# The last feed-forward's routing and sends moved into the attention ahead of it, its shared expert moved beside the gathers

## What is computed

```
# L3 attention: two mambas, one over the reversed sequence
u, z = split(x @ in_w.T);  u = silu(conv(u));  dbc = u @ xproj_w.T
dt = softplus(dbc[:64] @ dt_w.T + dt_b);  Bm, Cm = dbc[64:80], dbc[80:96]
h = exp(dt * A) * h + (dt * u) * Bm        # over time, 256 channels x 16 states
y = (h . Cm + u * D) * silu(z) @ out_w.T
# L3 feed-forward: 16 experts, 2 per token, at most CAP = 640 tokens each
probs = softmax(x @ router_w + router_b);  vals, idx = top_k(probs, 2)
pos = place of the token in its expert's queue;  within = pos < CAP
out = x + mlp(x, shared) + sum_k vals_k * within_k * mlp(rows, expert idx_k)
mlp(h) = (silu(h @ wg) * (h @ wu)) @ wd     # 176 hidden features
```

## Time and profile before

| | us |
|---|---|
| median of 3 runs | 3957.37 (3955.27 to 3960.35) |
| the profiled execution | 3963.04 |
| its span, first to last instruction | 3961.3 |
| PE busy | 3420.1 (86%), granted clock 0.943 of full |
| DVE, ACT, POOL busy | 2411.4 (61%), 1850.6 (47%), 1703.2 (43%) |
| last attention | 2589.0 to 3537.1 |
| last feed-forward | 3538 to 3943.2 |

### The profile page before, as it was taken

One profiled execution on the slowest core, in us unless ns is written; L12 is line 12 of the kernel. 1 busy time (PEld: TensorE's weight loads), 2 busy tenths in 40 slices (PEclk: granted clock), 3 DMA queues, 4 the chain that ended last, 5 costly groups with the idle time before them and its releaser, 6 DMA issues. The chain is left out here.

```text
span 3961.3 us, 70814 instructions
## 1 busy us (share of the span) xinstructions
PE 3420.1 (86%) x24832; PEld 2293.2 (58%) x24832; DVE 2411.4 (61%) x5406; ACT 1850.6 (47%) x5019; POOL 1703.2 (43%) x1869
## 2 busy tenths in 40 slices
PE   6888897769999899999988999879999999973781
PEld 3555554547777566666653444357777777762560
DVE  3788843446666556666643444458888888863233
ACT  4666655466666444454450000266666666620220
POOL 2555522337777633333310000146676667645106
PEclk7999998889999999999998999989999999986895
DMA  4888730030000000000016877512222222241112
GB/s 134 211 215 213 205 90 10 6 68 1 1 2 2 1 1 2 2 1 2 2 44 139 154 150 153 111 51 77 76 76 71 79 76 76 71 133 46 48 68 63
DMA packets 266184, 289.98 MB, mean 73 GB/s; under 512 B 60841, under 2 KB 177513, under 8 KB 265578
## 3 DMA queue, kind: packets, MB, share of 16 engines
q1 hardware_dynamic: 259146, 271.80, 27.5%
q0 software_dynamic: 4096, 8.40, 0.7%
q10 hardware_dynamic: 2592, 5.26, 0.3%
HBM read 233.21 MB, written 52.17 MB: 72 GB/s over the span
## 5 line engine op out<-in xcount | busy, mean ns | idle before, releaser
L2232 DVE TENSOR_TENSOR_SCAN a_h<-a_dA,a_dBu_psum 128x512 f32<-128x512 f32 x512 | 595.9, 1205 | 162.6 <-issue 105.9
L2189 POOL TENSOR_TENSOR a_h<-a_h,main_g 128x512 f32<-128x512 f32 x256 | 383.6, 1501 | 269.6 <-DVE a_h L2232 259.5
L1237 POOL TENSOR_SCALAR a_probs<-a_probs,a_row_inv 128x128 f32<-128x128 f32 (+1 forms) x512 | 380.0, 763 | 178.0 <-DVE a_row_inv L1200 178.0
L1703 DVE SCALAR_TENSOR_TENSOR m_hidden<-m_h_psum,m_gate_spread 128x512 f32<-128x512 f32 x256 | 176.8, 691 | 264.7 <-PE m_h_psum L1641 252.2
L1956 PE MATMUL a_dBu_psum<-a_B_diag,a_dt_u_turned 64*128 64x128 f32 x4096 | 316.9, 289 | 20.5 <-DVE a_h L2232 19.7
L1506 POOL TENSOR_TENSOR r_position_q<-r_turned_q 128x512 f32<-128x512 f32 x128 | 159.7, 1268 | 389.3 <-DVE r_turned_q L1551 389.3
L179 POOL TENSOR_TENSOR main_g<-main_g,main_s 128x512 f32<-128x512 f32 x28 | 41.2, 1503 | 632.1 <-ACT main_g L161 632.1
L1956 PEld LDWEIGHTS a_dBu_psum<-a_B_diag,a_dt_u_turned 64*128 64x128 f32 x4096 | 257.8, 188 | 74.5 <-issue 69.5
L1463 ACT ACTIVATE r_probs<-r_logits_psum,r_neg_max 128x256 f32<-128x256 f32 x512 | 235.0, 475 | 140.0 <-DVE r_neg_max L1557 140.0
L1142 ACT ACTIVATE a_probs<-a_logits,a_neg_max 128x128 f32<-128x128 f32 (+1 forms) x512 | 226.7, 446 | 127.0 <-DVE a_neg_max L1186 127.0
L1977 PE MATMUL a_y_psum<-main_ident,a_h 128*128 128x128 f32 x2048 | 274.9, 276 | 7.7 <-POOL a_h L2189 6.6
(11 more groups left out here) (519 smaller groups left out, 7659.0 us busy)
## 6 DMA issues: line engine op xcount, KB each, us to landing
m_gate_spread<-m_gate_rows SPq DMA_DIRECT2D x64, 1024.0 KB, 8.3
main_g<-a_b_c_rows SPq DMA_DIRECT2D x256, 256.0 KB, 3.1
a_band_rows<-main_g SPq DMA_DIRECT2D x64, 512.0 KB, 3.7
a_B<-a_band_rows SPq DMA_DIRECT2D x192, 128.0 KB, 3.4
a_A<-a_band_rows SPq DMA_DIRECT2D x192, 128.0 KB, 3.2
f_x_rows<-f_zero ACTq DMA_DIRECT2D x16, 320.0 KB, 8.6
f_x_expert<-f_x_rows SPq DMA_DIRECT2D x16, 320.0 KB
f_y_rows<-f_y_expert SPq DMA_DIRECT2D x16, 320.0 KB, 2.2
```

Source lines behind the costliest of these rows:

```text
L1237: ins = nc.gpsimd.tensor_scalar(pr[:, h % NPR, tile[t]], pr[:, h % NPR, tile[t]], rinv[:, p % NST, q:q + 1], None, ALU.mult)
L2189: tt(h[:, r, :, :], h[:, r, :, :], Cs[:, g % NCS, :, :], ALU.mult).then_inc(hc_pool, 1)
L2232: nc.vector.tensor_tensor_scan(flat, dA[:, M % NDA, q, k, :, :].rearrange("p n t -> p (n t)"), db[:, 2 * (g % 2) + k, :], 0.0, ALU.mult, A ...
```

## The change

Routing moves ahead. The router's logits are made by PE at the end of `gate_and_norm`, behind its last tile; picking and placing are DVE's first work in the attention block, ahead of the first scan; their tables lie in buffers that the attention needs from its second unit on. PE turns the tokens there, and SP writes them to DRAM (`x_tok`). SP clears the slots and reads the tokens back tile by tile, and POOL issues one send in three steps from step 26 on. The product with B's weights (`b_proj`) becomes `turn_b`, which turns B from `low`, the copy that ACT has made of the projection.

In the feed-forward the experts come first, with weights loaded in parts of four experts, and the rows of the next chunk are turned before the products of this one. The 16 shared chunks stand last; after every second one, DVE combines four tiles of gathered rows. The third layer's `rpe_bias` is loaded before SP's other loads.

```diff
@@ -245,9 +245,16 @@
+                    if beside and "tensor" in beside:
+
+                        pe.wait_ge(logged, N)
+                        for k in range(N):
+                            pe.wait_ge(normed, k + 1)
+                            beside["tensor"](pe, k, *own)
...
+                also("sync_first", sp)
@@ -976,8 +983,10 @@
...
+            def load(sp, rpe_in, *_):
+                sp.dma_start(rb[:], d["rpe_bias"]).then_inc(rpe_in, 16)
             def spread(sp, rpe_in, zeroed, padded, summed, ready, rows_out, bias_in, *_):
-                sp.dma_start(rb[:], d["rpe_bias"]).then_inc(rpe_in, 16)
...
+        def table(a):
+            return a.rearrange("p (t e) -> p t e", t=NT)
+        probs, eq = table(dt[1][:, 0, :]), table(dt[1][:, 1, :])
+        chosen = [table(dtu[1][:, k, :]) for k in range(TOPK)]
+        run = [table(zs[1][:, k, :]) for k in range(2)]
+        both, slot = (table(dtuT[1][:, q, :, :].rearrange("p c e -> p (c e)")) for q in range(2))
...
+            nc.vector.tensor_tensor(probs, table(rt[:, 0, :]), rb[:].unsqueeze(1).broadcast_to([P, NT, E]), ALU.add)
...
+        def router_logits(pe, k, weights_in, A_exp, flip_zero, log_mm):
+            if k == 0:
+                pe.wait_ge(weights_in, 16 * len(pairs))
+            for n in range(4 * k, 4 * k + 4):
+                ins = nc.tensor.matmul(rt[:, 0, n * E:(n + 1) * E], xn[:, n * P:(n + 1) * P], rw[:], start=True, stop=True,
+                                       skip_group_check=True)
+            if n == NT - 1:
+                ins.then_inc(log_mm, 1)
...
+        FIRST_CLEAR, FIRST_SCATTER, EVERY = 2, 26, 3
...
-                def b_proj(N):
+                def turn_b(N):
...
+                    pe.wait_ge(low_sb, N + 1)
                     for q in range(2 * TC):
-                        for k in range(NK):
-                            ins = mm(pj[:, 1, q * NS:(q + 1) * NS], u[:, k, q * P:(q + 1) * P],
-                                     W[N % 2]["xp"][:, k, DR:DR + NS], start=k == 0, stop=k == NK - 1)
+                        ins = mm(pj[:, 1, q * NS:(q + 1) * NS], low[:, q * P:(q + 1) * P],
+                                 c["ident"][0:DR + 2 * NS, DR:DR + NS], start=True, stop=True)
...
@@ -1965,6 +2024,8 @@
                     if m == 0:
                         if U:
                             pe.wait_ge(gated, 2 * (U - 1) + q + 1)
+                        else:
+                            pe.wait_ge(counted, 1)
...
+                def turn_tokens(m):
+                    if m >= 4:
+                        pe.wait_ge(lo_taken, m - 3)
+                    for n in range(4):
+                        ins = nc.tensor.transpose(db[:, m % 4, n * P:(n + 1) * P], xn[:, (4 * m + n) * P:(4 * m + n + 1) * P],
+                                                  c["ident"][:])
+                    ins.then_inc(turned_mm, 1)
+
+                def count():
+                    pe.wait_ge(picked, 1)
+                    flat = both.rearrange("p t e -> p (t e)")
+                    mm(yT[:, 0, :], c["earlier"][:], flat, start=True, stop=True)
+                    mm(yT[:, 1, :], c["ones"][:], flat, start=True, stop=True).then_inc(count_mm, 1)
...
+                for m in range(4, NG4):
+                    turn_tokens(m)
                 low_proj(0)
-                b_proj(0)
+                turn_b(0)
...
+                count()
+                pe.wait_ge(hi_taken, NG4 - 4)
...
+                def put_tokens(half):
+                    sp.wait_ge((lo_taken, hi_taken)[half], 4)
+                    src = h[:, 4 * half:4 * half + 4, :, :].rearrange("p r n t -> p (r n t)").rearrange("p (n f) -> p n f", f=P)
+                    sp.dma_start(x_tok[16 * half:16 * half + 16].rearrange("n p f -> p n f"),
+                                 src).then_inc((tokens_lo, tokens_hi)[half], 16)
+
+                def clear(e):
+
+                    sp.dma_start(route.slots(route.x_rows, e),
+                                 zero[:].unsqueeze(1).broadcast_to([P, PER, P])).then_inc(cleared, 16)
+                def take_row(n):
...
+                    if n >= NROW:
+                        sp.wait_ge(scattered[n % NROW], 16 * TOPK * (n // NROW))
+                    sp.dma_start(rows[:, n % NROW, :], x_tok[n]).then_inc(row_in[n % NROW], 16)
+
+                put_tokens(0)
...
+                    if g == NCS:
+                        put_tokens(1)
                     read_c(g)
+                    if FIRST_CLEAR + NCS <= g < FIRST_CLEAR + NCS + E:
+                        clear(g - FIRST_CLEAR - NCS)
+                    ahead = g - FIRST_SCATTER + 2 * TOPK * EVERY
+                    if ahead >= 0 and ahead % (TOPK * EVERY) == 0 and ahead // (TOPK * EVERY) < NT:
+                        take_row(ahead // (TOPK * EVERY))
...
+                def scatter(i):
+                    n, k = i // TOPK, i % TOPK
+                    if i == 0:
+                        pool.wait_ge(cleared, 16 * E)
+                    pool.wait_ge(row_in[n % NROW], 16 * (n // NROW + 1))
+                    nc.gpsimd.indirect_dma_start(route.x_rows, bass.IndirectOffsetOnAxis(ap=dest_u[:, n, k:k + 1], axis=0),
+                                                 rows[:, n % NROW, :], None).then_inc(scattered[n % NROW], 16)
...
                     times_c(g)
+                    if g >= FIRST_SCATTER and (g - FIRST_SCATTER) % EVERY == 0 and (g - FIRST_SCATTER) // EVERY < NT * TOPK:
+                        scatter((g - FIRST_SCATTER) // EVERY)
...
+                def pick():
+                    link(reduce(out=first[:], in_=probs, axis=AX_X, op=ALU.max))
+                    link(tt(probs, probs, per_tile(first[:]), ALU.subtract))
...
+                    tt(both, chosen[0], chosen[1], ALU.add).then_inc(picked, 1)
...
                     dve.wait_ge(dbu_mm, 2 * (g + 1))
+                    if g == 0 and k == 0:
+                        dve.wait_ge(tokens_lo, 16)
+                    if g == 2 and k == 0:
+                        dve.wait_ge(tokens_hi, 16)
...
+                pick()
+                for m in range(4, NG4):
+                    take_tokens(m)
+                place()
...
+                def turn(i):
+                    e, t, n = chunks[i]
+                    if t == 0:
+                        pe.wait_ge(x_in, 16 * (e + 1))
+                    if i >= 2:
+                        pe.wait_ge(turn_sb, i - 1)
+                    for k in range(n):
+                        ins = nc.tensor.transpose(tr[:, i % 2, k * P:(k + 1) * P], xe[:, e % NX, t + k, :], c["ident"][:])
+                    ins.then_inc(turn_mm, 1)
 
...
+                    if t == 0 and (e % PART == 0 or e == E):
+                        pe.wait_ge(loaded[e // PART], 16 * 3)
+                    if i < NSL:
+                        pe.wait_ge(turn_sb, i + 1)
+                        rhs = xeT[:, i % NXT, 0:w]
+                    else:
                         rhs = xn[:, t * P:t * P + w]
...
+                def turn_back(m):
+                    if m >= 2:
+                        pe.wait_ge(added, m - 1)
+                    for n in range(4 * m, 4 * m + 4):
+                        pe.wait_ge(combined, n + 1)
+                        ins = nc.tensor.transpose(tr[:, m % 2, (n % 4) * P:(n % 4 + 1) * P], acc[:, n % NG, :], c["ident"][:])
+                        ins.then_inc(back_mm, 1)
+
+                turn(0)
                 for i in range(NCH + 1):
+                    if i + 1 < NSL:
+                        turn(i + 1)
                     if i < NCH:
                         raise_(i)
                     if i >= 1:
                         lower(i - 1)
+                        if quad(i - 1) is not None:
+                            turn_back(quad(i - 1))
...
+                def combine(n):
+                    dve.wait_ge(gathered[n % NG], 16 * TOPK * (n // NG + 1))
+                    if n >= NG:
+                        dve.wait_ge(back_mm, n - NG + 1)
...
+                def add(m):
+                    dve.wait_ge(back_mm, 4 * m + 4)
+                    dve.wait_ge(o_sb, NSL + 2 * m + 2)
...
+                        m = quad(i - 1)
+                        if m is not None:
+                            for n in range(4 * m, 4 * m + 4):
+                                combine(n)
+                            if m >= 1:
+                                add(m - 1)
...
+                def load(part):
+                    es = slice(part * PART, (part + 1) * PART)
...
+                load(0)
                 for e in range(E + 2):
                     if e < E:
                         take_rows(e)
+                    if e % PART == 0 and e // PART + 1 < E // PART:
+                        load(e // PART + 1)
+                    if e == E - PART:
+                        load_shared()
                     if e >= 2:
                         put_rows(e - 2)
```

388 lines of the change are left out of this document (180 added, 208 removed).

## The result

The changed kernel takes 3869.38 us (3866.61 to 3872.01, 4 runs), the kernel before beside it 3958.86 (3955.27 to 3964.64): a ratio of 0.9773, 95% interval 0.9756 to 0.9789. It is faster, as forecast, but by half of what was forecast: the profiled spans are 3867.0 and 3961.3 us, a gain of 94.3 for 193, and 3869 lies outside the range of 3732 to 3812. Of the runs further on, one execution of `free_steps_again` took 8374.27 us at a granted clock of 0.413; it is left out of that kernel's ratio, but not of its median.

A forecast was written before the change was run, and what follows sets the result against it. PE was taken to bound the last attention, a serial DVE chain or POOL's indirect DMAs the routing, sends and gathers. Terms summed to -193.2 on the profiled 3963.0, so 3769.8, less 5.7 for the median: 3764 us, range 3732 to 3812.

The forecast's parts named there:

- Part 6: Last attention: 64 sends beside the scans, 16 of them in POOL's way at 0.6 us each; +9 us (0 to +40).
- the upper end of 40: Last attention: worst case for the sends beside the scans, +40 us, half of the 80.6 they add on POOL.
- Rival (b): Last attention: sends are on the path, any slip of POOL passed on; 80.6 us rather than 9, total 3835; chance 0.08.
- Rival (c): Last attention: each send holds up ACT and DVE some 11 us, 717 us added, about 4470, slower than before; chance 0.03.
- Parts 2 to 5: Third layer's load first -14 us, last norm +4.5, way to the first scan +12.5, B turned from ACT's copy -14.7.
- part 4: Way to the first scan: picking hidden in DVE's idle; PE's chain 29.8 us, then placing 14.0, scan at 44.2; +12.5 us.
- Rival (d): Before the first scan: routing isn't hidden as DVE's picking starts late; +31 us rather than +12.5, total 3783; chance 0.07.
- The experts' period: Feed-forward: an expert takes 7.1 us in place of 9.12, since turning one chunk ahead removes PE's waits; 16 take 113.8.
- Part 1: Feed-forward after the attention: 126.7 us until the first gather, gathers 88 with the shared expert hidden, tail 18.1; -190.5 us.
- rival (a): Gather stretch: PE at half clock beside the gathers, period 13.5 us, stretch 111 in place of 88, total 3787; chance 0.17.

The follow-up runs named there:

- free_steps_again: Changed kernel with sends ahead of POOL's product with C at steps 1, 3, 5, 7, 9, gathers as changed, run again for comparison: 3773.09 us, ratio 0.9574.
- sends_free_steps: Changed kernel with sends moved ahead of POOL's product with C, at steps 1, 3, 5, 7, 9 from the third unit on: 3789.36 us, ratio 0.9565.

## Why the prediction was right in sign and wrong in size

*Part 6, the sends beside the scans, is the step that failed.* It asked where a send stands in POOL's way, and priced 16 of the 64 at 0.6 us. That question was answered rightly as far as POOL goes: the memset in the send's place costs 13.5, not far from 9. It never asked what a send does to an instruction of DVE that starts beside it. The trace of before had no such pair with POOL going straight on: beside its gathers DVE's second combining instruction (L2559), with two inputs in SBUF, starts while an indirect DMA is issued in 30 of 32 tiles and takes its 0.35 us in all of them, but POOL stands still for some 0.30 us behind every gather. So the upper end of 40 ("the latter half of the 80.6") was a bound for the wrong mechanism. The cost is 82.6, and it isn't spread: 26 of 256 products carry 78 us more than their usual time, and over the attention PE stands still 49 us longer and, at a lower clock, works 34 us longer. The forecast had no term for either.

*Rival (b)* had the right size (80.6, total 3835) and 0.08, for another reason: POOL's load. `sends_free_steps` tells them apart, with POOL at 77% and no loss. *Rival (c)* spoke of stalls of other engines by single sends, with 3.2 us a send as the point where the change turns slower. 82.6 / 64 = 1.3 is well under it, so the sign was safe. What I held against it, that the first nine sends delayed nothing, looked at ACT and DVE instructions that read PSUM; the held ones read SBUF only.

The Trainium skill, "SBUF — State Buffer", section "Who interferes with whom", has a rule that bears on this: a DVE instruction with two inputs in SBUF contends with a GpSimd instruction that reads SBUF. Of DVE's two-port modes it says that whoever issues first has the shared ports for the whole instruction and blocks the other. The 1.71 beside the memset's follower agrees with both. The measured holds behind a send go further: they last for a whole run of POOL's instructions (4.25 us over three). The held one-input multiplication may or may not be a case of the rule, since the section counts `tensor_scalar` among the operations that can take both ports; in turned order it takes 0.68 us in the median, against 0.43 for one of the same size in plain order (2618.43 in the changed kernel). I had not brought the rule to bear, and it would have asked the right question.

*Parts 2 to 5* came out within 1.7 us each: -13.0, +6.0, +13.4, -13.0 (part 4's own terms, 29.8 and 14.0, add up to 43.8 and not to its 44.2). Rival (d) is out: DVE's picking was hidden in the idle before the scans, and only placing stood bare. Two errors nearly cancelled there. PE's chain was through 26.8 us after the start for the 29.8 I wrote, and placing took from 2608.8 to 2627.1, 18.3 us for 14.0. The reason is in single rows, of the kernel before and of the changed one:

```profile
3583.01 0.17 DVE L2503 COPY f_running<-f_running 128x16 f32<-128x16 f32 x1
```

```profile
2609.61 1.16 DVE L2406 COPY a_silu_z<-a_silu_z 128x16 f32<-128x16 f32 x1
...
2617.04 0.29 DVE L2406 COPY a_silu_z<-a_silu_z 128x256 f32<-128x256 f32 x1
```

The same small copy takes 1 us more while POOL works (on dt and the first diagonals, to 2616.6), and the next three take 0.8 to 1 us more (1.13, 0.97, 1.00); the fifth, behind POOL's run, is at its 0.29 of before. The section just named counts copies among the operations that can contend with POOL, and here the trace agrees. The experts' period was 7.44 for 7.1.

*Part 1, the gathers*: the floor was right and the reading of the stretch was not. Where handoffs are on time, the 64 gathers, unchanged, take 85.2 to 86.4 us in four profiles, with the lower clock in it, for the 88 forecast:

```profile
3748.00:3834.00 86.00, 59.97 (x202) 39.04 (x200) 39.42 (x102) 8.30 (x14) 61.48 (x64) 0.81 0.19 49
```

(the changed kernel, run again). PE is at 0.81 there, the pairs of chunks start with four gate matmuls of 1.37 to 1.91 us for 1.03, and the 10 us of POOL hide it: rival (a)'s mechanism is there and costs nothing. The 12.2 us over the forecast in the first profile come from the late handoffs that the earlier trace rows had shown at the sends. I had argued them away for the gathers because none showed beside those of before, where ACT and PE hand nothing to each other that could be late. Why the handoffs were late stays open: the runs say that the same kernel has them in some sets of runs and not in others, and no more.

By the sum: 75.3 from the sends, 12.2 from the gathers, 5.5 before the first gather, and 5.9 from the small terms together, of a miss of 98.9.

## What to carry to other kernels

An indirect DMA put beside a tuned pipeline can cost more than its own time on POOL, if POOL goes straight on behind it while DVE starts on data in SBUF: put it where POOL must wait anyway, here ahead of a product that waits for DVE. Move it with the data of one period in hand, step by step, and look at the longest instructions of the *other* engines, not at the mean or the load. And before a cure is judged, the unchanged kernel is run beside it on the same chip, since a delay of 27 us was there in some sets of runs and not in others.

## What the runs showed of the hardware

- A product of DVE (0.67 us) that starts while POOL issues an indirect DMA, or in the unbroken run of POOL instructions behind it, ended some 0.56 us after that run: 2.80 to 6.97 us in the changed kernel. A memset of 1.06 us in the DMA's place gives at most 1.80; a one-column memset behind it leaves as many (27 long for 26 and 27); behind a standstill of 0.07 us or more none was held; one input in place of two, in turned order, does not help (31 long).
- Where PE stood still for 3.86 us behind a held product, the granted clock was 0.68 and 0.75 in the next two stretches of 3 us, and four matmuls of 512 columns took 3.49 us for 1.98. Over the attention this adds 34 us to PE's busy time (881.7 for 847.7).
- A small copy of DVE in SBUF (128x16) takes 0.17 us alone and 1.16 beside a working POOL. An indirect DMA takes POOL 0.97 us alone and 1.03 beside the attention.
- Beside unbroken runs of indirect DMAs, handoffs from PE to ACT and on to DVE came 2 to 6 us late beside the gathers and up to 18 beside the sends of the kernel before (its gate matmuls end at 3648.9, ACT starts at 3666.8), in three sets of runs, and not at all in three others, with the same kernel. With a pause after every four sends they were on time on a chip that otherwise had them late.
